# Thirty-two landing slots instead of sixteen for the gathered rows of three of four message passes

## The reference

```
h  = relu(layernorm(x))
# pass 0: GCN.  deg, dinv = rsqrt(deg)
h  = segment_sum((h @ W1)[src] * dinv[src] * dinv[dst], dst) + b1
h  = h / max(norm(h), 1e-12)
# pass 1: gated sum over edges
ev = sigmoid(h[src] @ We1[:H] + h[dst] @ We1[H:] + be1)
na = relu(segment_sum(ev * h[src], dst) @ Wn1 + bn1)
# pass 2: the same with We2; the gates ev2 are kept
ev2 = sigmoid(na[src] @ We2[:H] + na[dst] @ We2[H:] + be2)
g  = relu(segment_sum(ev2 * na[src], dst) @ Wn1 + bn1)
# pass 3: GCN with edge weights ev2
out = x + gcn_conv(g, src, dst, ev2, W2, b2)
```

## Time and profile before

| | us |
|---|---|
| median of 3 runs | 3395.2 (3388.78 to 3397.36) |
| the profiled execution | 3382.53 |
| its span, first to last instruction | 3380.7 |
| granted TensorE clock, mean | 0.916 of full speed |
| pass 0, first gather to last pair matmul | 130.3 to 999.6 |
| pass 1 | 1109.0 to 1774.0 |
| pass 2 | 1873.9 to 2630.5 |
| pass 3 | 2688.0 to 3354.5 |

### The profile page before, as it was taken

How to read it: one execution, slowest core, us unless ns; L and a number is a source line. 1 busy time by engine, 2 the same in 40 slices (tenths; PEclk the granted TensorE clock), 3 DMA queues, 4 the chain that set the end, 5 groups by cost and what they waited for, 6 DMA issues and landing times.

```text
span 3380.7 us, 58791 instructions
## 1 busy us (share of the span) xinstructions
PE 2650.3 (78%) x16470; PEld 2298.0 (68%) x16470; DVE 2111.6 (62%) x6199; ACT 1617.7 (48%) x3249; POOL 1847.0 (55%) x1816
## 2 busy tenths in 40 slices
PE   0566667898898677777789899999999767777765
PEld 0334434888886566666778788888888666666765
DVE  5556666666654466666675566666666456666667
ACT  7146655666666455555464444444444422223222
POOL 5444335556503666766640566666662267766773
PEclk9678888999999789889899999999999878898898
DMA  4233434555542333333331444444442433333333
GB/s 113 70 106 145 157 141 152 208 214 192 216 172 89 102 112 100 99 112 99 113 96 56 132 135 133 133 135 133 134 133 88 137 99 96 98 112 98 112 100 93
DMA packets 185804, 419.58 MB, mean 124 GB/s; under 512 B 36865, under 2 KB 136910, under 8 KB 175743
## 3 DMA queue, kind: packets, MB, share of 16 engines
q10 hardware_dynamic: 83703, 244.23, 20.4%
q0 software_dynamic: 61472, 140.49, 15.2%
q1 hardware_dynamic: 40328, 31.23, 3.0%
HBM read 311.35 MB, written 102.16 MB: 122 GB/s over the span
## 4 chain that ended last, share of the span: by engine, by line
PE 65%; issue 12%; DVE 10%; ACT 3%; ACTq 3%; another core or an unknown queue 3%; DMA 2%; DVEq 1%; SPq 1%; POOL 0%; POOLq 0%
PE ps L1119 18%; PE ps_high L1111 16%; PE ps_high L1119 12%; PE ps L1058 6%; PE ps_high L1076 3%; PE ps L1042 3%; ACT tab_area L770 2%; PE ps_high L1071 2%; ACTq L377 2%; DVE acc L1596 2%; PE ps_high L1198 1%; DVE weights L1572 1%; DMA acc<-counts 1%; DVE tab_area L1523 1%
## 5 line engine op out<-in xcount | busy, mean ns | idle before, releaser
L602 POOL DMA_INDIRECT rows<-table,edge_src x1664 | 1742.7, 1047 | 1213.0 <-SPq L496 682.3
L1111 PE MATMUL ps_high<-rows,weights 128*128 x2784 | 648.6, 343 | 381.5 <-issue 222.0
L1119 PE MATMUL ps<-tab_area,acc 128*128 128x129 f32 (+2 forms) x4410 | 823.5, 327 | 7.8 <-issue 7.7
L1111 PEld LDWEIGHTS ps_high<-rows,weights 128*128 128x128 f32 x2784 | 475.9, 205 | 480.4 <-issue 281.9
L1119 PEld LDWEIGHTS ps<-tab_area,acc 128*128 128x128 f32 x4410 | 699.4, 207 | 52.8 <-issue 8.7
L864 ACT ACTIVATE step<-xbuf,rows 128x128 f32 x928 | 357.4, 394 | 673.4 <-PE ps_high L1111 320.9
L1596 DVE TENSOR_TENSOR acc<-acc 128x640 f32<-128x640 f32 x735 | 604.8, 823 | 104.0 <-ACT acc L873 60.5
L1119 PE MATMUL ps_high<-tab_area,acc 128*128 128x129 f32 (+2 forms) x2940 | 587.8, 325 | 0.8 <-issue 0.7
L1579 DVE TENSOR_TENSOR acc<-acc,ps_high 128x129 f32 (+1 forms) x948 | 335.1, 353 | 376.4 <-PE ps_high L1111 190.6
L770 ACT ACTIVATE tab_area<-ps_high x816 | 404.1, 495 | 346.9 <-issue 162.8
L1119 PEld LDWEIGHTS ps_high<-tab_area,acc 128*128 128x128 f32 x2940 | 477.0, 205 | 30.2 <-issue 2.2
(11 more groups left out here) (242 smaller groups left out, 2173.1 us busy)
## 6 DMA issues: line engine op xcount, KB each, us to landing
acc<-counts ACTq DMA_DIRECT2D x105, 1120.0 KB
counts<-tab_area ACTq DMA_DIRECT2D x51, 1568.0 KB
acc<-counts ACTq DMA_DIRECT2D x25, 1568.0 KB
rows<-table,edge_src POOLq DMA_INDIRECT x1664
table<-tab_area SPq DMA_DIRECT2D x6, 903.0 KB, 5.2
table<-acc SPq DMA_DIRECT2D x7, 448.0 KB, 4.1
table<-tab_area SPq DMA_DIRECT2D x6, 455.0 KB, 4.1
table<-tab_area SPq DMA_DIRECT2D x6, 448.0 KB, 3.0
```

Source lines behind the costliest of these rows:

```text
L602: nc.gpsimd.indirect_dma_start(rows[:, t % UNROLL, 0:row_floats[k]], None, tables[k], bass.IndirectOffsetOnAxis(ap=edge_src[:, t:t + 1], a ...
L1111: nc.tensor.matmul(ps[DENSE_BANKS + m % PAIR_BANKS][:, 0:WIDTH[k]], weights[:, m % W_RING, :], rows[:, bass.ds(known["slots"][m % UNROLL], ...
L1119: ins = nc.tensor.matmul(ps[j][:, 0:WIDTH[k]], gate_blocks[:, n % S_RING, j * PART:(j + 1) * PART], table[:, h, 0:WIDTH[k]], start=(h == 0 ...
```

## The change

Passes 0, 1 and 3 get 32 slots of 128, 130 and 128 words; pass 2, with rows of 258 words, keeps 16. The tile `rows` becomes 32 x 130 words (4160 for 4128), with a view for each pass, `rows_of[k]`. POOL's wait is for edge tile t - 32 in these passes. There are 32 semaphores `landed` instead of 16; room for them is made by letting others share: `disorder_sent`, `first_sent` and `low_sent` become `flags_sent` with counts 1, 2, 3; the four `tab_stored` become one that counts on; `fin_scaled` is counted on `pool_scaled`. The slot numbers in `pair_row` are (edge tile) and 31; DVE makes them anew with and 15 in the middle stage ahead of pass 2, and with and 31 again behind it, ahead of pass 3.

```diff
+SLOT_RING = 32
+ROW_RING = (SLOT_RING, SLOT_RING, UNROLL, SLOT_RING)
...
-        rows = sb("rows", [PART, UNROLL, ROW])
+        rows = sb("rows", [PART, SLOT_RING * ROW1])
...
+        rows_of = [within(rows, 0, [ROW_RING[k], row_floats[k]]) for k in range(4)]
...
-        tab_ready, tab_stored = [sem(f"tab_ready{k}") for k in range(2)], [sem(f"tab_stored{k}") for k in range(4)]
+        tab_ready, tab_stored = [sem(f"tab_ready{k}") for k in range(2)], sem("tab_stored")
...
-        landed = [sem(f"landed{u}") for u in range(UNROLL)]
+        landed = [sem(f"landed{u}") for u in range(SLOT_RING)]
...
+        def landed_count(k, t):
+            slot = t % ROW_RING[k]
+            earlier = sum(HALF // ROW_RING[q] for q in range(k) if slot < ROW_RING[q])
+            return 16 * (earlier + t // ROW_RING[k] + 1)
...
-                        sp.wait_ge(landed[u], tiles_before(k) + 16 * (i + 1))
+                        sp.wait_ge(landed[(i * UNROLL + u) % ROW_RING[k]], landed_count(k, i * UNROLL + u))
...
-                pool.wait_ge(tab_stored[k], 16 * (NODE_TURNS if k == 0 else len(PIECES)))
+                pool.wait_ge(tab_stored, 16 * (NODE_TURNS + k * len(PIECES)))
                 for t in range(HALF):
-                    if t >= UNROLL:
-                        pool.wait_ge(slots_free, tiles_before(k) + t - UNROLL + LAG + 1)
-                    nc.gpsimd.indirect_dma_start(rows[:, t % UNROLL, 0:row_floats[k]], None, tables[k],
-                                                 bass.IndirectOffsetOnAxis(ap=edge_src[:, t:t + 1], axis=0)).then_inc(landed[t % UNROLL], 16)
+                    if t >= ROW_RING[k]:
+                        pool.wait_ge(slots_free, tiles_before(k) + t - ROW_RING[k] + LAG + 1)
+                    nc.gpsimd.indirect_dma_start(rows_of[k][:, t % ROW_RING[k], :], None, tables[k],
+                                                 bass.IndirectOffsetOnAxis(ap=edge_src[:, t:t + 1], axis=0)).then_inc(landed[t % ROW_RING[k]], 16)
...
-            chain(single(pair_row[:, 1, :], pair_row[:, 2, :], 15.0, ALU.add))
-            chain(single(pair_row[:, 1, :], pair_row[:, 1, :], UNROLL - 1, ALU.bitwise_and))
+            def row_slots(ring):
+                chain(single(pair_row[:, 1, :], pair_row[:, 2, :], float(ring - 1), ALU.add))
+                chain(single(pair_row[:, 1, :], pair_row[:, 1, :], ring - 1, ALU.bitwise_and))
+            row_slots(SLOT_RING)
...
             for j in range(diag_lead):
                 diagonal(j)
-            v.wait_ge(tab_stored[1], 16 * len(PIECES))
+            row_slots(UNROLL)
+            v.wait_ge(tab_stored, 16 * (NODE_TURNS + len(PIECES)))
...
             nc.vector.tensor_single_scalar(stat[:, 0, :], acc3[:, 0:NODE_TILES, ONE], 1.0, ALU.add).then_inc(sqrt_need, 1)
+            row_slots(SLOT_RING)
             rooted(2)
```

More of the change, by code:

```diff
@@ L239, in gnn_kernel @@
         below = within(spare_sums, 2 * GROUP * PART, [2, GROUP, PART])
-        between = rows[:, :, :].rearrange("p a b -> p (a b)")
+        between = rows[:, :]
+        rows_of = [within(rows, 0, [ROW_RING[k], row_floats[k]]) for k in range(4)]
         staged = within(between, 0, [GROUP, HID])
@@ L860, in gate @@
                     if m % UNROLL == 0:
-                        known[m // UNROLL] = [load_pairs(SCA, k, part, m // UNROLL, top) for part, top in ((0, SPARE), (1, UNROLL - 1), (2, HALF))]
+                        known[m // UNROLL] = [load_pairs(SCA, k, part, m // UNROLL, top) for part, top in ((0, SPARE), (1, ROW_RING[k] - 1), (2, HALF))]
                     node, slot, need = (column[m % UNROLL] for column in known[m // UNROLL])
@@ L864, in gate @@
                     ins = act.activation(gates[:, m % G_RING, :], xbuf[:, bass.ds(node, 1), :].rearrange("p o f -> p (o f)"),
-                                         ACT.Sigmoid, bias=rows[:, bass.ds(slot, 1), SOURCES[k]])
+                                         ACT.Sigmoid, bias=rows_of[k][:, bass.ds(slot, 1), SOURCES[k]])
                     if m >= W_RING:
@@ L947, in _ @@
             pe.wait_ge(disorder_ready, 1)
-            nc.tensor.matmul(ps[5][0:1, 0:1], disorder, ones[:, 0:1], start=True, stop=True).then_inc(disorder_sent, 1)
+            nc.tensor.matmul(ps[5][0:1, 0:1], disorder, ones[:, 0:1], start=True, stop=True).then_inc(flags_sent, 1)
             pe.wait_ge(unsorted_ready, 1)
@@ L967, in _ @@
                 last = nc.tensor.matmul(ps[h][:, 0:TABLE // 2], ones[0:1, :], first[0][:, h * (TABLE // 2):(h + 1) * (TABLE // 2)], start=True, stop=True)
-            last.then_inc(first_sent, 1)
+            last.then_inc(flags_sent, 1)
             pe.wait_ge(half_ready, 1)
-            nc.tensor.matmul(ps[6][:, 0:1], ones[0:1, :], half_f[0:1, 1:2], start=True, stop=True).then_inc(low_sent, 1)
+            nc.tensor.matmul(ps[6][:, 0:1], ones[0:1, :], half_f[0:1, 1:2], start=True, stop=True).then_inc(flags_sent, 1)
             pe.wait_ge(ld_const, 64)
@@ L1042, in multiply @@
                     ins = nc.tensor.matmul(ps[m % FIRST_BANKS][:, 0:FEAT], weights[:, m % (2 * QUAD), :],
-                                           rows[:, bass.ds(first_pass.slots[u], 1), 0:FEAT].rearrange("p o f -> p (o f)"), start=True, stop=True)
+                                           rows_of[0][:, bass.ds(first_pass.slots[u], 1), 0:FEAT].rearrange("p o f -> p (o f)"), start=True, stop=True)
                     if m >= FIRST_BANKS:
@@ L1104, in multiply @@
                     if m % UNROLL == 0:
-                        known["slots"] = load_pairs(TEN, k, 1, m // UNROLL, UNROLL - 1)
+                        known["slots"] = load_pairs(TEN, k, 1, m // UNROLL, ROW_RING[k] - 1)
                         if k == 3:
@@ L1111, in multiply @@
                     nc.tensor.matmul(ps[DENSE_BANKS + m % PAIR_BANKS][:, 0:WIDTH[k]], weights[:, m % W_RING, :],
-                                     rows[:, bass.ds(known["slots"][m % UNROLL], 1), 0:WIDTH[k]].rearrange("p o f -> p (o f)"),
+                                     rows_of[k][:, bass.ds(known["slots"][m % UNROLL], 1), 0:WIDTH[k]].rearrange("p o f -> p (o f)"),
                                      start=True, stop=True)._wait_ge(weights_ready, weights_before(k) + m + 1).then_inc(pairs_done[k], 1)
```

24 lines of the change are left out of this document (12 added, 12 removed).

## The result

The changed kernel takes 3443.0 us (3441.4 to 3446.4, 4 runs) beside 3394.5 us for the kernel before (3388.8 to 3397.4, 4 runs): ratio 1.0146, 95% interval 1.0129 to 1.0164. It is 48.5 us slower. The forecast was 17 us slower, 3412 in a range from 3368 to 3440, so its sign was right and its size wrong; the time lies 3 us outside the range. The profiled execution of the changed kernel has a span of 3439.6 us, 58.9 more than that of the kernel before (3380.7). That is more than 48.5 because the profiled execution before was 12 us quicker than its median.

What follows compares the result with a forecast made beforehand. Prediction: PE's news of finished pairs, late while POOL issues gathers, holds up the readers, not landings. Ends -18, starts of passes 1 and 3 +26, pass 0 +8, slot numbers +0.7: +16.7, forecast 3412 us, range 3368 to 3440.

Steps and rivals of the forecast that it cites:

- Reading of the bound: Steady passes: gathers already ahead of readers; DVE waits for PE's news of pairs, late while POOL issues without pause.
- Part 1: Ends of passes 1 and 3: about 17 more pairs run without gathers beside them, -18 us, bounds 0 and -18.
- the last rival: Readers bound by gathers after all, short slot waits in the path of two passes: 3260 us, chance 0.05.
- Part 2: Starts of passes 1 and 3: 16 more unpaced gathers, 20 us holding 5 pairs instead of 14, +13 each, +26 us.
- Part 3: Start of pass 0: POOL's first pause comes 16 gathers later, first 32 pairs end near 200, +8 us.
- Parts 4 and 5: Slot numbers remade ahead of passes 2 and 3, 0 and +0.7 us; merged semaphores with added-up counts, 0.
- The sum: Whole kernel: -18 + 26 + 8 + 0.7 = +16.7 us on the profiled execution's 3382.5; median forecast 3412.
- no progress in the longer run: Rival: readers stand altogether in the 20 us more at pass starts, +42 us, 3437, chance 0.11.
- Gather-bound: Rival: slot waits stand in the readers' path, 68 us in each of two passes, 3260 us, chance 0.05.
- The signs: Changed profile: first pause after 38 or so gathers, under 14 records in 1129:1149, gather-free stretch 30 us longer, steady pairs 1.43 us.
- The two rules weighed: Issuing DMAs early: already satisfied, up to 21.4 us of landings; POOL and DVE contending for SBUF: 0, 823 against 820 ns.

Runs made afterwards that it cites:

- f5: Changed kernel, waited values through max(value, 0), 16 gathers ahead until gather 96 of passes 0, 1, 3, then 32: 3444.1 us beside 3391.1 for the kernel before.
- f1: Changed kernel, waited values through max(value, 0), 16 ahead rising by steps to 32 in passes 0, 1, 3: 3438.8 us beside 3393.1 for the kernel before.
- f2: Changed kernel with its 32 slots, waited values through max(value, 0), only 16 gathers ahead in every pass: 3404.2 us beside 3392.5 for the kernel before.
- b3: Changed kernel, its waited values passed through max(value, 0), nothing else altered, slow session: 3452.4 us beside 3391.4 for the kernel before, ratio 1.0188.
- f3: Changed kernel, waited values through max(value, 0), only 8 gathers ahead in all four passes: 3744.8 us beside 3368.3 for the kernel before.
- f4: Changed kernel, waited values through max(value, 0), 8 ahead rising by steps to 16 in all four passes: 3361.9 us beside 3369.0 for the kernel before.
- b1: Changed kernel, its waited values passed through max(value, 0), nothing else altered, quick session: 3215.1 us beside 3214.2 for the kernel before, ratio 0.9996.
- f6: Kernel before with 16 slots, 8 ahead rising by steps to 16, waited values loaded as 16-bit halves: 3486.3 us beside 3392.2 for the kernel before.

## Why the prediction was wrong

The forecast's mechanism stood, that readers lose while POOL runs without a pause. The sizes of two of its terms did not, parts 2 and 3.

- **Reading of the bound.** "A deeper ring only lets them be further ahead" was right, and so was that the readers suffer from POOL's unbroken runs. What I passed over is what follows from how busy POOL is. In the steady part of pass 1 a gather takes 1.513 us, of which POOL is occupied 1.35, or 89%; I used these numbers for the last rival alone. A chain with POOL at 0% hides this: the chain names the wait that ended last, and that was PE's late news.
- **Part 1, the ends: about right.** Forecast -18. Pass 1: the kernel before is at its 401st pair 593.6 us after its first gather and at its last pair after 664.8; the changed kernel 618.6 and 683.8. That is 6.0 us shorter; in pass 3, by the same count, 8.3 us. Together -14. (For pass 3 I took 1.44 us a pair where the row gives 1.466; that changes 0.4 us.)
- **Part 2, the starts: the step that failed, in its size.** I let the readers do 5 pairs in the 20 us more. They did about none. The windows 1156:1176 and 1176:1196, which hold that run and its wake, have 5 pairs in 40 us, and in 200 us 113 pairs against 126. Up to pair 128 pass 1 lost 24.9 us and pass 3 23.1: +48 where I had +26. The standstill lasts as long as POOL's run and some 6 us longer, so its price is not less than the 16 gathers' own 20 us. The trace of the kernel before could have told: I read two pairs in 11.7 us from the earlier trace rows, but between these rows stands a third pair and then nothing at all for 10 us:

```profile
1125.88 0.49 PE L1111 MATMUL ps_high<-rows,weights 128*128 x2
1136.48 0.80 PE L1111 MATMUL ps_high<-rows,weights 128*128 x2 [10.11 <-issue]
```

  Seen from POOL: by my numbers pass 1's last gather should have come 17 x 1.436 - 13 = 11 us sooner after the first; it came 3.1 us sooner.
- **Part 3, pass 0: failed likewise.** +27.4 for +8. I counted only the first 32 pairs and let them be slowed; they were stopped (158 records in the first 200 us of the pass against 180). The 32nd came 15.8 us later, and by the 128th it was 28.8.
- **Parts 4 and 5: right.** 0.7 forecast; pass 2 and the stages between the passes moved by 0.6 us at most.
- **The sum.** -14 + 48 + 27 = +61, for 58.9 of span measured and 48.5 of median. The rival "no progress in the longer run", with 0.11 the fourth in order, gave +42 and was the one that came nearest; its mechanism is what the timeline shows. That the forecast named the right sign rests on the same reading and is not luck; it would have failed in a quick session, a kind that neither the forecast nor its rivals considered.
- **Gather-bound** was excluded because no landing is waited for. In the quick sessions passes 1 and 3 are paced by POOL (1.346 us a gather), and depth does nothing there either.
- **The signs.** POOL's first pause came after 39 gathers, 49 us into the pass (forecast 38 and 48), the second 20 us had 4 records (forecast fewer than 14), and 1207:1487 has 194 pairs, 1.443 us each (forecast 1.43). The stretch without gathers grew by 22 us, not 30; by my own part 1 it should have been 17 x 0.93 = 16.
- **The two rules weighed.** No more landings are waited for than before (18.6 us in all), and the block multiply beside gathers takes 823 ns again.

What the experiments add is that the start is not special (f5). In pass 1, f1, f5 and f2 all issue 183 gathers in a steady 280 us, and in passes 1 and 3 the last gather comes 630 to 636 us after the first in the kernel before, the changed kernel, b3, f1, f2 and f5, whether 16 or 32 ahead. What POOL is let ahead it does in place of pauses, and in its pauses the readers move. Sixteen gathers more ahead cost 21 to 25 us there by the 128th pair (f1, f5 and b3 against f2), by steps or at once, and 7 to 10 come back at the end.

How late the news comes goes with how long POOL runs without a pause, and with the kind of session. For pass 1, worked out from the records: the longest run of gathers (pauses up to 0.6 us not counted), and the longest time from a pair's last matmul record to its addition; some 5 us of it stand in the quick sessions too.

| pass 1 | f3 | f4 | f2 | before | f1 | f5 | b3 | after | all eleven quick ones |
|---|---|---|---|---|---|---|---|---|---|
| gathers without a pause | 8 | 17 | 21 | 22 | 21 | 24 | 38 | 39 | 416 |
| addition after its pair, us | 5.3 | 6.8 | 14.7 | 15.3 | 14.5 | 25.8 | 37.8 | 37.5 | 4.7 to 6.4 |

The run's length alone doesn't make the standstill, though. In pass 3 of f1 POOL issues 39 gathers from 3240.5 to 3296.3 without a pause, and the readers keep their pace (81 records, 40 pairs, 1.4 us each):

```profile
3240.50:3296.30 55.80, 15.39 (x81) 12.05 (x80) 0.87 0.36 107
```

Of these gathers 17 take 1.29 us and more, where nearly all of those of the standstills take 0.94 to 1.01. What makes the difference no run shows.

In pass 0 a gather's turn is longer, as the gathers of the kernel before show in a window of it:

```profile
838.00:938.00 100.00, 57.09 (x58) 0.98 0.56 204
```

That is 1.72 us, of which POOL is occupied 0.98 and 0.30. It has pauses to spare, and there the steps cost 2 us (f1) and the jump 15 (f5). That POOL's occupancy is the cause of this difference is argued from these two passes, not shown by a run of its own. It doesn't explain f4's passes 1 and 3, 11 and 8 us shorter than f2's though both end 16 ahead; the shorter run at their starts does for 8.7 and 8.0.

Two things stay open. Why PE's count reaches its waiters late while POOL issues, in slow sessions alone: the instructions of POOL, DVE and ACT have the same durations in both kinds (in the kernel before and b1 a gather takes 944 and 945 ns at the median, DVE's block multiply 823 and 822 in the mean, ACT's block of gates 819 and 820), and no run here takes the cause apart. And what makes a session slow: the two kinds differ by 5.5% for the same kernel (3392 and 3214), far more than the change.

## What to carry to other kernels

Slots are of use only where a landing is waited for and the producer is held up by full slots; count both waits first. In the slow sessions the first was missing (5 landings waited for), in passes 1 and 3 of the quick ones the second (653 landings waited for, and no pause of POOL), and depth was of no use in either. Before letting a producer run further ahead, add up how much of each turn it is occupied: where readers stand while it issues, as in the slow sessions here, the distance must be built up once in each pass, at the producer's full price if it has no time to spare, and is paid back at the end only by as much as readers are quicker without it. Where the trace shows readers that stand still during an unbroken run of a producer, take the whole of a longer run as lost at such a place, not a share of it. And run a change beside the kernel before in more than one session: here the same change cost 1.5% in one kind and nothing in the other.

## What the runs showed of the hardware

- PE's count of finished pairs reached ACT, DVE and SP up to 38 us late while POOL issued 39 indirect DMAs without a pause, 5.8 us after the last of them. In the eleven quick profiles no addition of pass 0 came more than 1.7 us after its pair, under runs of 48 to 92 gathers, and none of pass 1 more than 6.4, under 416 without a pause. In the slow kind too one run of 39 (f1, pass 3) went by without a standstill.
- SP's own increments, 0.017 us at the median, took 0.4 us and more (0.52 to 0.70 at the median of these) 46 to 114 times in 3328 in eight slow profiles, 4 times in the ninth (f3, 8 ahead), and never in the eleven quick ones.
- A load of 16 values with a stride, as 16-bit halves, took 3.25 us on SP where 16 adjacent words took 0.97, and f6, which has them, was 2.9% slower than the kernel before.
